# Shared tiles in pairs 6 to 21, routing spread over twelve slots, three scatters a slot, and weighted rows added in 128x512 pieces

## What is computed

```python
def attention(x):                     # x is the normed input, 8 x 512 x 128
    scores = einsum('bqhif,bkhif->ibhqk', qs, ks) * scale        # two maps
    atts = softmax(scores)
    o = einsum('bhqk,bkhe->bqhe', atts[0] - diff_weight * atts[1], vs)
    return (o * rms(o) * norm_w) @ Wo.T ...
def ffn(x):
    gates = sigmoid(x @ Wg); vals, idx = top_k(gates, 2); vals /= vals.sum()
    shared = silu(x @ Ws1) * (x @ Ws3) @ Ws2
    routed = sum over the two experts of  w * (silu(x @ We1) * (x @ We3)) @ We2
    return (shared + routed) / 3
return x + attention(xn) + ffn(xn)
```

## Time and profile before

| | |
|---|---|
| median of 3 runs | 591.58 us (591.34 to 592.21) |
| the profiled execution | 593.5 us, of which the span from first to last instruction is 591.4 us |
| PE busy | 563.0 us, 95% |
| DVE busy | 469.2 us, 79% |
| ACT busy | 401.8 us, 68% |
| POOL busy | 218.2 us, 37% |
| mean granted TensorE clock | 0.983 of full |
| DMA | 74.07 MB, mean 125 GB/s |

### The profile page before, as it was taken

One profiled execution on the slowest core, in us unless ns is written; L12 is line 12 of the kernel. 1 busy time (PEld: TensorE's weight loads), 2 busy tenths in 40 slices (PEclk: granted clock), 3 DMA queues, 4 the chain that ended last, 5 costly groups with the idle time before them and its releaser, 6 DMA issues.

```text
span 591.4 us, 13553 instructions
## 1 busy us (share of the span) xinstructions
PE 563.0 (95%) x4688; PEld 335.1 (57%) x4688; DVE 469.2 (79%) x1012; ACT 401.8 (68%) x808; POOL 218.2 (37%) x296
## 2 busy tenths in 40 slices
PE   7797999999999999999999999999999999999993
PEld 6565545555555554555665665566556655665442
DVE  5989778888888896778878787887878788878195
ACT  4463575767667666777777777777677777777781
POOL 5630063555655554123323233332333233332310
PEclk9898898999999999999999999999999999999998
DMA  6997400260116222485435834476344844420292
GB/s 181 206 154 151 110 6 15 55 150 29 37 37 151 59 84 58 133 215 179 130 109 150 264 111 122 130 203 196 116 144 128 231 140 150 130 83 14 66 298 81
DMA packets 62531, 74.07 MB, mean 125 GB/s; under 512 B 7296, under 2 KB 42496, under 8 KB 62464
## 3 DMA queue, kind: packets, MB, share of 16 engines
q1 hardware_dynamic: 57952, 64.00, 42.1%
q0 software_dynamic: 4352, 8.95, 4.7%
q10 hardware_dynamic: 160, 0.26, 0.2%
HBM read 40.08 MB, written 15.80 MB: 94 GB/s over the span
## 4 chain that ended last, share of the span: by engine, by line
PE 67%; DVE 14%; issue 7%; DMA 3%; ACT 3%; POOL 3%; SPq 2%; POOLq 0%; DVEq 0%; ACTq 0%
PE O L1167 15%; PE T L1138 10%; PE F L1207 9%; DVE rowmax L846 7%; PE F L1221 6%; PE F L1204 5%; PE T L1143 4%; PE F L1101 2%; PE O L1128 2%; PE F L1186 2%; DMA yt<-ysb,xst 2%; SPq L264 1%; DVE base L938 1%; PE O L1033 1%; DVE base L924 1%
## 5 line engine op out<-in xcount | busy, mean ns | idle before, releaser
L652 ACT ACTIVATE probs<-T 128x512 f32<-128x512 f32 x372 | 202.7, 597 | 94.9 <-PE T L1143 61.7
L846 DVE TENSOR_REDUCE rowmax<-S 128x1 f32<-128x512 f32 x370 | 237.9, 682 | 27.9 <-PE S L1128 25.9
L1128 PE MATMUL S<-kop,qop 32*128 32x512 f32 x370 | 140.5, 454 | 3.4 <-DVE rowmax L846 2.1
L1167 PE MATMUL O<-probs,vop 128*32 128x512 f32 x1024 | 124.1, 601 | 0.2
L486 POOL DMA_INDIRECT yt<-ysb,xst x72 | 72.1, 1001 | 136.6 <-DMA yt<-ysb,xst 119.7
L1138 PE MATMUL T<-qop,kop 32*128 32x512 f32 x372 | 99.4, 498 | 1.4 <-ACT probs L652 1.0
L1143 PE MATMUL T<-mop,ones_r 2*128 2x512 f32 x372 | 78.3, 399 | 0.0
L475 POOL DMA_INDIRECT xs<-xn,slot_i x64 | 62.5, 977 | 42.1 <-DVE rowmax L846 26.1
L652 ACT ACTIVATE probs<-V 128x512 f32<-128x512 f32 x126 | 76.5, 607 | 1.9 <-PE S L1143 1.9
L1207 PEld LDWEIGHTS F<-xsT,wrt_all 128*128 128x128 f32 x576 | 67.0, 191 | 13.3 <-issue 8.8
L1207 PE MATMUL F<-xsT,wrt_all 128*128 128x128 f32 x576 | 73.9, 281 | 0.5
(11 more groups left out here) (168 smaller groups left out, 879.1 us busy)
## 6 DMA issues: line engine op xcount, KB each, us to landing
wrt_all<-in_wexp SPq DMA_DIRECT2D x72, 384.0 KB, 3.9
qop<-qparts SPq DMA_DIRECT2D x64, 128.0 KB
kop<-kparts SPq DMA_DIRECT2D x62, 128.0 KB
xs<-xst SPq DMA_DIRECT2D x12, 387.0 KB, 7.9
xst<-xs SPq DMA_DIRECT2D x36, 129.0 KB, 3.9
base<-in_x SPq DMA_DIRECT2D x8, 256.0 KB, 4.8
xn<-yt SPq DMA_DIRECT2D x8, 256.0 KB, 4.8
out_x<-base SPq DMA_DIRECT2D x7, 256.0 KB, 3.8
```

What stands on the lines that cost most here:

```text
L652: A(probs[:, n % NP, :], banks[e_bank[n]][:, :], ACT.Exp, scale=SCALE).then_inc(s_p, 1)
L846: V.reduce_max(rowmax[hf][:, x_map[n], c, x_row[n]:x_row[n] + 1], banks[x_bank[n]][:, :], AX).then_inc(s_mx, 1)
L1128: mm(banks[x_bank[n]][:, :], qop[b % 2][at:at + BAND, c, t * P:(t + 1) * P], kop[b % 2][at:at + BAND, c, :], start=True, stop=True, tile_p ...
L1167: last = mm(O[VW * j:VW * (j + 1), :], vop[b % 2][:, t, (4 * g + j) // MAPS, :], probs[:, n % NP, :], start=(t == 0), stop=(t == QT - 1), ...
```

## The change

1. Shared tiles move from pairs 4 to 19 into pairs 6 to 21. Bare pairs are now 0 to 5 and 58 to 63 (before: 0 to 3, 20, 21, 58 to 63). `keep_busy` runs 24 a pair in pairs 0 to 5, 12 in pair 58, and none in pairs 59 to 63: 156 in all in bare pairs, before 192.
2. Routing steps on DVE stand behind every second maximum at first; the weights come before the counts (steps 14 to 18), and the last seven steps stand behind four maxima of pair 5. The prefix sum is in pair 3. POOL's steps are at slots 7 and 9.
3. Scatters go three a slot from slot 12, so over slots 12 to 33.
4. A row carries its weight as word 130. `copy_y` becomes two activations of 128x128 that scale each row by it, so `yt` holds weighted rows.
5. A partition holds four neighbouring tokens of a batch ("(p t)" in place of "(t p)"), so loads, gathers and stores of a batch have runs of 2 KB where they had 512 bytes. `load_y` is one DMA a batch, `combine` two plain additions of 128x512.

```diff
-    SH_AT = [8 + 2 * i for i in range(SH_TILES)]
+    SH_AT = [12 + 2 * i for i in range(SH_TILES)]
...
-    PREFIX_AT = 2
-    SCAT0 = 10
+    PREFIX_AT = 3
+    SCAT0, SCATS = 12, 3
+    FILL_TO, HEAVY = 59, 6
...
-    W = D + 1
+    W = D + 2
...
-        R_DVE = {n: n for n in range(14)} | {19: 28, 20: 29} | {n: n + 5 for n in range(29, 41)}
-        R_POOL = {n: 4 if n < 19 else 6 for n in (14, 15, 16, 17, 18, 21, 22, 23, 24, 25, 26, 27, 28)}
+        R_DVE = {n: 2 * n if n < 14 else n + 13 for n in range(19)} | {24: 36, 25: 37} | {n: 46 + (n - 34) // 2 for n in range(34, 41)}
+        R_POOL = {n: 7 if n < 24 else 9 for n in (19, 20, 21, 22, 23, 26, 27, 28, 29, 30, 31, 32, 33)}
...
-                for k in range(TOPK):
-                    at = TOKENS * k + SEQ * b
-                    sp.dma_start(gbuf[b][:, k, :, :], yt[at:at + SEQ, :].rearrange("(t p) d -> p t d", p=P)).then_inc(s_g[b], 16)
+                rows = yt[0:TOPK * TOKENS, :].rearrange("(k b p t) d -> b p k (t d)", k=TOPK, b=BATCH, p=P)
+                sp.dma_start(gbuf[b].rearrange("p k t d -> p k (t d)"), rows[b]).then_inc(s_g[b], 16)
...
+                G.tensor_scalar(xn[:, :, D + 1], wts[:, k, :], 1.0, None, ALU.mult).then_inc(s_ids, 1)
...
-                    for i in range(2):
+                    for i in range(SCATS):
                         if scat < TOPK * NT:
-                            gp.wait_ge(s_mx, 4 * (slot + LEAD) + 3 + 2 * i)
+                            gp.wait_ge(s_mx, 4 * (slot + LEAD) + 3 + i)
...
-                A(ysb[r % 2][:, :, :].rearrange("p s d -> p (s d)"), F[1][:, 0:TOK], ACT.Copy).then_inc(s_yc, 1)
+                for i in range(2):
+                    A(ysb[r % 2][:, i, :], F[1][:, i * P:(i + 1) * P], ACT.Copy, scale=xst[r % NX][:, i, D + 1:W]).then_inc(s_yc, 1)
...
                 for k in range(TOPK):
-                    for t in range(QT):
-                        if k:
-                            dve.wait_ge(s_cmb, 8 * b + t + 1)
-                        row = base[:, QT * b + t, :]
-                        V.scalar_tensor_tensor(out=row, in0=gbuf[b][:, k, t, :], scalar=wts[:, k, QT * b + t:QT * b + t + 1],
-                                               in1=row, op0=ALU.mult, op1=ALU.add).then_inc(s_cmb, 1)
+                    if k:
+                        dve.wait_ge(s_cmb, TOPK * b + k)
+                    V.tensor_tensor(rows, rows, gbuf[b][:, k, :, :], ALU.add).then_inc(s_cmb, 1)
...
-                if bare(p):
-                    keep_busy(16 if p < 4 else 8, ["F1"])
+                if bare(p) and p < FILL_TO:
+                    keep_busy(16 if p < HEAVY else 8, ["F1"])
```

More of the change, by code:

```diff
@@ L325, in load_y @@
                     sp.wait_ge(s_st, 4 * QUADS * (BATCH - 1))
-                for k in range(TOPK):
-                    at = TOKENS * k + SEQ * b
-                    sp.dma_start(gbuf[b][:, k, :, :], yt[at:at + SEQ, :].rearrange("(t p) d -> p t d", p=P)).then_inc(s_g[b], 16)
+                rows = yt[0:TOPK * TOKENS, :].rearrange("(k b p t) d -> b p k (t d)", k=TOPK, b=BATCH, p=P)
+                sp.dma_start(gbuf[b].rearrange("p k t d -> p k (t d)"), rows[b]).then_inc(s_g[b], 16)
             def store_out(n):
-                sp.wait_ge(s_cmb, 8 * (n + 1))
-                sp.dma_start(out[n].rearrange("(t p) d -> p t d", p=P), base[:, QT * n:QT * n + QT, :]).then_inc(s_out, 16)
+                sp.wait_ge(s_cmb, TOPK * (n + 1))
+                sp.dma_start(out[n].rearrange("(p t) d -> p t d", p=P), base[:, QT * n:QT * n + QT, :]).then_inc(s_out, 16)
             def store_last(h):
@@ L336, in store_last @@
                 sp.wait_ge(s_pd, QT * n + t0 + 2)
-                sp.dma_start(out[n, P * t0:P * t0 + 2 * P].rearrange("(t p) d -> p t d", p=P),
+                sp.dma_start(out[n].rearrange("(p t) d -> p t d", p=P)[:, t0:t0 + 2, :],
                              base[:, QT * n + t0:QT * n + t0 + 2, :]).then_inc(s_out, 16)
@@ L471, in scatter @@
                     row_ids(k)
-                    gp.wait_ge(s_ids, k + 2)
+                    gp.wait_ge(s_ids, 2 * k + 3)
                 if n >= 2:
@@ L932, in combine @@
                     dve.wait_ge(s_pd, QT * (b + 1))
+                rows = base[:, QT * b:QT * b + QT, :]
                 for k in range(TOPK):
-                    for t in range(QT):
-                        if k:
-                            dve.wait_ge(s_cmb, 8 * b + t + 1)
-                        row = base[:, QT * b + t, :]
-                        V.scalar_tensor_tensor(out=row, in0=gbuf[b][:, k, t, :], scalar=wts[:, k, QT * b + t:QT * b + t + 1],
-                                               in1=row, op0=ALU.mult, op1=ALU.add).then_inc(s_cmb, 1)
+                    if k:
+                        dve.wait_ge(s_cmb, TOPK * b + k)
+                    V.tensor_tensor(rows, rows, gbuf[b][:, k, :, :], ALU.add).then_inc(s_cmb, 1)
             for e in range(E):
```

73 lines of the change are left out of this document (37 added, 36 removed).

## The result

The changed kernel took 616.36 us (median of four executions, 614.25 to 618.53), the kernel before 591.89 beside it: the ratio is 1.040, 95% interval 1.036 to 1.044. I had forecast 584.2, in a range of 580 to 589.5. It is 24 us slower, and the time stands outside the range on the other side. The profiled execution has a span of 615.1 us, before 591.4.

What follows compares the result with a forecast made beforehand. The prediction took the attention frame on PE, 67% of the chain, to set the time. Its terms, -1.9 -2.9 +0.6 +0.2 +0.7 +0.5 -1.75 -2.8, summed to -7.35, so 591.58 became 584.2 us, range 580 to 589.5.

Steps and rivals of the forecast that it cites:

- Opening, -1.9: Pairs 0 to 3: moved reciprocal and fewer early DVE routing steps save 1.9 us, bounds -0.7 and -2.7.
- Pair 4, -2.9: Pair 4, now bare with fillers, takes 7.46 us in place of 10.36: -2.9, bounds -1.5 and -3.3.
- Pair 5, +0.6, and pair 6, 0: Pair 5: seven routing steps behind four maxima make it 9.4 us, +0.6, bounds 0 and +1.5; pair 6 had no term.
- rival C: Front gives nothing: pair 5's steps hold DVE, pair 6's first shared tile is cold; 589.6 us, chance 0.12.
- Pairs 20 to 22, +0.2: Shared tiles in pairs 20 and 21 instead of bare pairs cost 0.2 us, bounds 0 and +0.5.
- POOL, +0.7: Three scatters a slot put POOL behind, so `rms_pow` of batch 1 is late for `add_proj`: +0.7 us, bounds 0 and +3.
- rival B: POOL backlog decides: `add_proj` in pair 19 waits 5 us, +4.3 or so more, 588.7 us; chance 0.14.
- copy_y, +0.5: ACT: two weighted activations a tile cost 0.28 us more over 36 tiles, nearly all hidden: +0.5, bounds 0 and +2.
- Tail on DVE, -1.75: Kernel end: 128x512 additions shorten combining, removing DVE's 1.8 us wait before the last reciprocal: -1.75, bounds -1.2 and -2.1.
- Tail on PE, -2.8: Pairs 59 to 63: removing twelve fillers, 0.93 us a pair, counted in three of five pairs: -2.8, bounds -4.2 and 0.
- rival A: Tail fillers stood in PE's waits for ACT and cost nothing, so removing them gains nothing: 587.0 us, chance 0.20.
- rival D: Pairs 59 to 63: without fillers the clock falls, costing 13 us in place of the 2.8 gain: about 600, chance 0.09.

Runs made afterwards that it cites:

- the first experiment: Changed kernel with three scatters a slot only in slots 12 to 15, two in later slots: 592.49 us, ratio to before 1.000.
- the sixth experiment: Kernel before with only the fillers of pairs 59 to 63 taken away: 596.29 us, ratio 1.0065.
- ninth experiment: Kernel before with only three scatters a slot in place of two (slots 10 to 31): 606.56 us, ratio 1.0267.
- the tenth experiment: Changed kernel with two scatters a slot from slot 16, tail fillers back, last seven routing steps one per maximum, combining in eight 128x128 additions a batch: 586.71 us.
- third: Changed kernel with three scatters in even slots and two in odd ones: 599.62 us.

## Why the prediction was wrong, point by point

For the terms that the POOL queue and the cold tail cover, the profile of the first experiment is used: it is the changed kernel without the queue, in an execution with a clock of 0.986. Its span was 7.2 us below that of before, where my sum was -7.35. That is luck: up to pair 58 it was 4.75 us ahead, where my terms give 2.8, and from there 2.46, where they give 4.55. It is also the fastest of ten executions, whose median is no better than before. Of the eight terms six erred by less than 2 us, one by 20, and the last was a loss where I had a gain.

- **Opening, -1.9:** `weigh` of pair 3 began at 81.41 there, -2.16. In the changed kernel's own execution it was 83.31, only -0.26: pair 1 took 8.63 us, and not 7.7. In both PE no longer waits behind the reciprocal (1.66 us before). Right in mechanism, within the spread of single executions.
- **Pair 4, -2.9:** 90.71 - 83.31 = 7.40 us, forecast 7.46. Right for this pair. But in the sixth and ninth experiments, whose opening is that of before, pair 4 took 8.57 and 8.75 where the earlier trace rows give 10.36. Their cold stretch came a pair earlier, at 81 to 84 us (clock 0.50 and 0.61), and pair 3 took 8.28 and 8.10 in place of 7.36. Pairs 3 and 4 together took 17.7 us before, 16.8 in these two, and 15.5 in the changed kernel: the gain is 1.4 to 2.2 us by execution. I had taken the place of the cold stretch in one profile for the rule.
- **Pair 5, +0.6, and pair 6, 0:** 8.02 and 8.68 us in the first experiment, -0.7 and +0.6. The steps behind four maxima didn't hold up pair 5, the hole came a pair later. Their sum is about nothing, where I had +0.6. In the profile of the changed kernel pair 6 took 11.26 with the clock at 0.50, as rival C has it.
- **Pairs 20 to 22, +0.2:** 24.63 against 24.39. Right.
- **POOL, +0.7 with a bound of +3, rival B with +5:** it was +20.8. The failed step is "What stands behind the scatters is `rms_pow` of batch 1 (slot 36)". That was the second deadline on the queue. The first is the `unpack` at slot 33, with a room of 8.8 us, and PE itself waits for it. I had walked POOL's order to a late arrival of up to 220 and looked only at one reader. The size of the step was short too: 1.53 us a scatter is the pace in one run of eight; from the `unpack` at 107.67 to that at 217.74 it was about 1.63, with the other instructions taken off, and from `unpack` to `unpack` 22.0 us went by, where four slots last 16.5. That is 1.4 us of delay a slot, and I had "half a us a slot". And the price lacked what a stop of PE brings with it: 16.3 us of waiting cost 20.8. What the runs put in the place of this step is thus a wait of PE itself for `unpack`, and not the partly hidden one of `add_proj` in pair 19.
- **copy_y, +0.5:** this row is of the changed kernel, before it is 403 ns once:

```profile
L650 ACT ACTIVATE ysb<-F,xst 128x128 f32<-128x128 f32 x72 | 23.1, 382 | 4.9 <-PE F L1222 4.8
```

  ACT was busy 23.1 us with the 36 pairs, 0.64 us each, which is 0.24 more than 0.403; twice 382 ns is 0.76, as the two overlap. Pairs 24 to 57 show nothing of it. Pair 58 alone, where the fillers wait for the bank, took 0.24 us more. The cover was complete. The Trainium skill ("ScalarE: Activation LUTs", "What ACT_TABLE_LOAD costs") gives, as an estimate from its figures, 0.68 us for the pair with the overlap of neighbours taken off; the 0.64 of the row agrees within 6%.
- **Tail on DVE, -1.75:** the last additions, the copy and the last reciprocal of the first experiment:

```profile
566.10 3.30 DVE L940 TENSOR_TENSOR base<-base,kop 128x512 f32<-128x512 f32 x4
...
573.55 0.40 ACT L624 ACTIVATE o_all<-F 128x272 f32<-128x272 f32 x1 [0.81 <-PE F L1102]
...
573.98 0.25 DVE L891 RECIPROCAL o_inv<-o_all 128x16 f32<-128x16 f32 x1 [4.58 <-ACT o_all L624]
```

  The reciprocal began 0.03 us after the copy, before 1.82. The number is right; the reason given, instructions of 128x512, isn't, as the tenth experiment shows. Four of them took 3.30 us, and not the 2.7 that I took from the earlier trace rows.
- **Tail on PE, -2.8:** with a clock at 1.00 throughout, in the first experiment, it was -0.4, from `weigh` of pair 58 to the copy (29.81 against 30.20 us). That is rival A: the pairs got shorter (25.09 against 26.54), but pair 63 then waited for ACT's exponentials instead. And in most executions it was a loss, the mechanism of rival D, with a chance of 0.09. The failed step is "so I count three of five: 3 x 0.93 = 2.8": it prices the fillers by their own length and the clock at nothing. The rival's direction was right. Its price, 13 us, was too high: the median of the sixth experiment lies 5.8 us above that of before beside it, and its longest execution some 10. I had argued against it that PE would still be busy 85% of the time. The clock fell behind a stretch where it was busy 3.33 of 4.

In the profile of the changed kernel the mechanisms of three rivals stand together: POOL's backlog (B, though at `unpack` and four times its price), the cold pair 6 (C) and the cold tail (D). I had given them separate chances, as if one excluded the other, and the range took in none of their sums. Two of their sums were off as well: B's 5 us in place of 0.7 give 588.5, and C's 589.6 counts the +0.6 twice, which leaves 589.0.

## What to carry to other kernels

When an in-order queue gets more work, list every consumer behind it with its deadline, not only the one that was tight before, and count every instruction on the queue against the time of a period: a delay adds up, costs nothing until the smallest room is used, and from there on costs at least its own length. A transfer paced by waiting for the one before last can be made cheaper by letting more be under way, with no less work. Filler matmuls that look like cost may carry the clock: take them out of the kernel before alone, and look at ten executions, not one.

## What the runs showed of the hardware

- A stop of PE cost more than its length: after 16.3 us without work the granted clock was 0.50 and stayed so over the next ten us, and the pair took 20.8 us more. Stops of 6.3 us (ninth experiment) and 3.9 us (third) made it 8.7 and 5.4 us longer.
- Two indirect DMAs under way gave one each 1.53 us back to back, and about 1.63 over the range; with four under way it was 1.28, and the last of 64 was sent 24 us earlier. POOL's own part is 0.96 us and some 0.3 between.
- On DVE the last additions of the combining took 829 ns each at 128x512 and 277 at 128x128, and four of the first took as long together as sixteen of the second (3.3 us).
- The same program has several times, by how many cold stretches it meets. The kernel before lay mostly between 588.6 and 592.2 (clock 0.976 to 0.984), and at 596 in four of 31 (0.969 to 0.970); without the tail's fillers it lay anywhere from 590.3 to 600.8.
